# Loads, first projections, bias step and vector code of the attention phase rearranged in a two-layer gated transformer kernel

## What is computed

```
x = x + tanh(g_xattn[0]) * attention16(layernorm(x), ctx)      # 16 heads of 8
x = x + tanh(g_ffn[0])   * moe_silu(layernorm(x))              # 8 experts, top 2
x = x + tanh(g_xattn[1]) * bidaf(layernorm(x), ctx)            # trilinear attention
x = x + tanh(g_ffn[1])   * lora_moe_gelu(layernorm(x))         # 8 experts, top 2
```

## Time and profile before

| | us |
|---|---|
| median of 3 runs | 536.44 |
| lowest and highest run | 534.65, 537.83 |
| span of the profiled execution, first to last instruction | 534.4 |
| attention phase, from the start to the last `a_rec` | about 224 |

### The profile page before, as it was taken

The page is one execution under the profiler, slowest core; times in us unless marked ns, Lnnn a source line. Parts: engine busy times, 40 slices in busy tenths (PEclk is TensorE's granted clock), DMA queues, the critical chain, the costliest instruction groups (busy, mean ns, idle before and its releaser), DMA issues. The chain is left out here.

```text
span 534.4 us, 14733 instructions
## 1 busy us (share of the span) xinstructions
PE 487.3 (91%) x4456; PEld 394.8 (74%) x4456; DVE 420.5 (79%) x1690; ACT 316.8 (59%) x777; POOL 234.2 (44%) x328
## 2 busy tenths in 40 slices
PE   2688999998999989989999999998998999989997
PEld 1366777776767767777888888775887888779897
DVE  4788899999999969777766667685779995777973
ACT  1567877677776667545566665557553557454553
POOL 3322255545555465543330366541458864224420
PEclk9999999899999999999999999999999999999999
DMA  9603011000100121125675344331000112000011
GB/s 245 277 11 91 21 36 32 29 29 29 34 29 29 38 72 41 36 68 158 178 207 165 104 131 118 89 95 36 21 27 20 45 47 69 12 0 1 2 41 39
DMA packets 48129, 36.85 MB, mean 69 GB/s; under 512 B 6466, under 2 KB 43970, under 8 KB 47812
## 3 DMA queue, kind: packets, MB, share of 16 engines
q1 hardware_dynamic: 31332, 21.13, 13.3%
q0 software_dynamic: 4640, 9.45, 6.2%
q10 hardware_dynamic: 12096, 5.51, 3.7%
HBM read 22.44 MB, written 13.63 MB: 67 GB/s over the span
## 5 line engine op out<-in xcount | busy, mean ns | idle before, releaser
L474 POOL DMA_INDIRECT yg<-done,gidx x64 | 64.4, 1007 | 40.2 <-PE bank L1604 17.8
L1638 PE MATMUL bank<-QK 128*64 128x256 f32 x512 | 70.8, 399 | 11.1 <-DVE Pr L909 5.7
L458 POOL DMA_INDIRECT sent<-xr,rowu x60 | 58.9, 981 | 43.2 <-DVE rowu L1014 22.0
L440 POOL TENSOR_TENSOR ve<-mv,half 128x4 f32<-128x4 f32 (+1 forms) x40 | 8.9, 222 | 122.5 <-DVE mv L826 121.5
L1205 DVE TENSOR_TENSOR act<-sil,bank 128x256 f32<-128x256 f32 x80 | 33.6, 420 | 33.5 <-ACT sil L667 33.2
L617 ACT ACTIVATE PT<-bank 128x512 f32<-128x512 f32 x64 | 36.4, 602 | 35.7 <-PE bank L1604 34.9
L1638 PEld LDWEIGHTS bank<-QK 128*64 128x64 f32 x512 | 32.5, 139 | 29.8 <-DVE Pr L909 8.7
L667 ACT ACTIVATE sil<-bank 128x256 f32<-128x256 f32 x80 | 30.8, 384 | 39.4 <-PE bank L1794 39.4
L1810 PE MATMUL bank<-f0w_s,aT 128*128 x320 | 50.0, 279 | 0.7 <-DVE yb L1211 0.6
L905 DVE TENSOR_REDUCE mx<-bank 128x8 f32<-128x512 f32 x64 | 43.7, 682 | 4.2 <-PE bank L1638 4.0
L909 DVE TENSOR_TENSOR Pr<-bank,mx 128x512 f32<-128x512 f32 x64 | 43.7, 683 | 1.2
(11 more groups left out here) (237 smaller groups left out, 1323.0 us busy)
## 6 DMA issues: line engine op xcount, KB each, us to landing
xb<-sent SPq DMA_DIRECT2D x80, 64.0 KB
done<-yb ACTq DMA_DIRECT2D x80, 64.0 KB
cT<-ctx_t_dram SPq DMA_DIRECT2D x16, 128.0 KB, 2.1
f0w_s<-f_w_dram SPq DMA_DIRECT2D x1, 2048.0 KB, 11.1
Pr<-ctx_t_dram SPq DMA_DIRECT2D x8, 256.0 KB
QK<-ctx_tok_dram SPq DMA_DIRECT2D x8, 256.0 KB
out_dram<-xs SPq DMA_DIRECT2D x8, 256.0 KB, 2.3
xs<-x_dram SPq DMA_DIRECT2D x2, 512.0 KB, 5.7
```

Of the source, the lines that this page charges most:

```text
L458: nc.gpsimd.indirect_dma_start(sent, bass.IndirectOffsetOnAxis(ap=rowu[:, s, 2 * k + c:2 * k + c + 1], axis=0), rows[:, c, :], None).then_ ...
L474: nc.gpsimd.indirect_dma_start(yg[:, s, j, :], None, done[u // (U4 // HALVES)], bass.IndirectOffsetOnAxis(ap=gidx[:, s, j:j + 1], axis=0)) ...
L1638: last = mm(bank[g % 2][L * b:L * (b + 1), 256 * p:256 * (p + 1)], QT[:, s, g, t:t + L], Kb[:, s, :, t:t + L], start=True, stop=True)
```

## The change

1. **Loads.** SP loads two tiles of `x` first instead of four, then the constants, the context columns of unit 0, the next two tiles, the context columns of unit 1, the gates, eight tiles, and then the other small ones and the last twenty tiles. A new semaphore `ld_first` covers the constants, the bias columns and the weights of K and Q. ScalarE's queue loads the bias columns, then the weights of K, Q, V and O. The router's weights move from GpSimd's queue to SP's.
2. **Statistics** of the first four tiles are taken two by two, and GpSimd makes two small steps of them. `norm` of units 0 and 1 stands ahead of the preparations (`first_norm`).
3. **K of unit 0** is projected into bank 7 as soon as `ld_first` is there. ScalarE evicts K (`first_keys`), copies the transposed tiles, and evicts Q (`first_queries`), raising a semaphore for each of the four instructions; each group of scores of unit 0 waits for its own. The tanh of the gates follows behind them, and VectorE's preparations wait for it.
4. **Products that are never read** (`unread`, 128x512 in bfloat16, bank 6) are put on TensorE: eight at the start, then two, two and three between the first steps.
5. **The bias step.** The product of value bias and output weight goes from the very start to iteration -1, ahead of the fourth group of scores, and `split_biases` from iteration -3 to the end of iteration -1.
6. **VectorE's iterations** -3 to 15 are all straight code; its hardware loop is gone. The other engines keep theirs.

```diff
-X_FIRST = (0, 4, 12, 20, CH)
+X_FIRST = (0, 2, 4, 12, CH)
...
+            x_load(0)
+            sp.dma_start(cst[:], consts).then_inc(ld_first, 16)
+            first_columns(0)
+            x_load(1)
+            first_columns(1)
+            sp.dma_start(gate[:], gates.partition_broadcast(P)).then_inc(ld_small, 16)
+            x_load(2)
+            sp.dma_start(rowv[:], rows.partition_broadcast(P)).then_inc(ld_small, 16)
+            sp.dma_start(farf[:], far).then_inc(ld_small, 16)
+            sp.dma_start(f0g_s[:], f0_wg).then_inc(ld_small, 16)
+            x_load(3)
...
-            for w_s, w in ((wq_s, wq), (wk_s, wk), (wv_s, wv), (wo_s, wo)):
-                a.dma_start(w_s[:], w).then_inc(ld_attn, 16)
-            a.wait_ge(ld_small, 80)
-            nc.scalar.activation(tg[:], gate[:, 0:4], ACT.Tanh).then_inc(prep_act, 1)
+            a.dma_start(colv[:], cols).then_inc(ld_first, 16)
+            for w_s, w, signal in ((wk_s, wk, ld_first), (wq_s, wq, ld_first), (wv_s, wv, ld_attn), (wo_s, wo, ld_attn)):
+                a.dma_start(w_s[:], w).then_inc(signal, 16)
+            a.wait_ge(ld_first, 64)
...
+            def first_keys():
+
+                a.wait_ge(prep_pe, 1)
+                a.wait_ge(prep, 1)
+                a_ks(0, bank[7][:, 0:2 * P])
+
+            def first_queries():
+
+                a.wait_ge(S("a_qk"), 1)
+                a.wait_ge(fill, 11)
+                for g in range(NG):
+                    a_qs(0, g).then_inc(prep_act, 1)
...
-            a.wait_ge(prep, 3)
-            a.wait_ge(fill, 11)
+            first_keys()
+            a_xts(0)
+            first_queries()
+            a.wait_ge(ld_small, 64)
+            nc.scalar.activation(tg[:], gate[:, 0:4], ACT.Tanh).then_inc(prep_act, 1)
...
+            first_tiles(0)
+            v.wait_ge(ld_first, 64)
             nc.vector.tensor_scalar(bkm[:], cst[:, C_KM:C_KM + HG], colv[:, BK:BK + 1], None, ALU.mult).then_inc(prep, 1)
+            first_tiles(1)
+            first_norm(0)
+            first_norm(1)
+            v.wait_ge(ld_small, 64)
+            v.wait_ge(prep_act, NG + 2)
...
-                if isinstance(u, int) and u == -3:
-                    split_biases()
...
+                if isinstance(u, int) and u == -1:
+                    split_biases()
...
-            pipelined(v, it_a, -3, 3, UT, UA)
+            for u in range(-3, UA):
+                it_a(u, u % 2)
...
+            pe.wait_ge(fill, 8)
+            unread(6, 8)
+            pe.wait_ge(ld_first, 64)
+            pe.wait_ge(ld_cT[0], 16)
+            a_k(0, bank[7][:, 0:2 * P]).then_inc(prep_pe, 1)
+            unread(6, 2)
+            a_xt(0, 0)
+            unread(6, 2)
+            pe.wait_ge(S("a_xts"), 1)
+            a_q().then_inc(S("a_qk"), 1)
+            unread(6, 3)
...
+                if isinstance(u, int) and u == -1:
+                    output_bias()
```

More of the change, by code:

```diff
@@ L319, in has, with begun @@
             return not isinstance(u, int) or 0 <= u < units
+        def begun(u):
+            return isinstance(u, int) and u <= -2
         def pipelined(eng, it, first, loop, behind, end):
@@ L345, in _, with x_load, first_columns @@
         def _(sp):
[L346 to L354, removed]
+            def x_load(i):
                 some = slice(X_FIRST[i], X_FIRST[i + 1])
                 sp.dma_start(xs[:, some, :], x_v[:, some, :]).then_inc(ld_x[i], 16)
+            def first_columns(s):
+                sp.dma_start(cT[:, s, 0:2 * P], ctx_t[:, 2 * P * s:2 * P * (s + 1)]).then_inc(ld_cT[s], 16)
+            x_load(0)
[9 more added lines that the diff above has]
+            x_load(3)
             sp.dma_start(f0w12_s[:], f0_w12).then_inc(ld_f0, 16)
@@ L475, in fetch @@
                                                  bass.IndirectOffsetOnAxis(ap=gidx[:, s, j:j + 1], axis=0)).then_inc(back_s[s], 16)
-            with pool.Fori(0, U4) as u:
+            for i in range(2):
+                two = slice(2 * i, 2 * i + 2)
+                pool.wait_ge(S("mv0"), 1 + 2 * i + 2)
+                nc.gpsimd.tensor_tensor(ve[:, 0, two], mv[:, 0, two, 1], half[:, 0:1].to_broadcast([P, 2]), ALU.add).then_inc(S("ve0"), 1)
+                pool.wait_ge(S("ve0"), i + 1)
+                nc.gpsimd.tensor_tensor(ln[:, two, 1], ve[:, 0, two], half[:, 2:3].to_broadcast([P, 2]), ALU.pow).then_inc(S("ln0"), 1)
+            with pool.Fori(1, U4) as u:
                 rstd(0, u, 4)
@@ L597, in a_xts, with a_qs, a_ks @@
                 nc.scalar.activation(xT[:, 0, 0:2 * P], bank[4][:, 0:2 * P], ACT.Copy).then_inc(S("a_xts"), 1)
+            def a_qs(s, g):
+                rows_g = slice(32 * g, 32 * (g + 1))
+                return nc.scalar.activation(QT[rows_g, s, g, :], bank[4][rows_g, 0:2 * P], ACT.Identity, bias=bqs[rows_g], scale=float(DH) ** -0.5)
+            def a_ks(s, keys):
+                for j in range(HG):
+                    last = nc.scalar.activation(Kb[:, s, j, :], keys, ACT.Identity,
+                                                bias=bkm[:, j:j + 1], scale=cst[:, C_KM + j:C_KM + j + 1])
+                return last
             def a_qks(u, s):
@@ L637, in it_a @@
                     a_ats(u - 1)
-                if has(u + 2):
+                if has(u + 2) and not begun(u):
                     a_xts(u + 2)
@@ L1126, in it_a @@
                     r_keep(u - 3, 1 - s)
-                if has(u + 3):
+                if has(u + 3) and not begun(u):
                     wait(v, S("a_xt"), u + 2)
```

86 lines of the change are left out of this document (49 added, 37 removed).

## The result

The changed kernel takes **543.7 us** (median of 4 runs, 542.2 to 544.6) against 535.7 in the same session (4 runs, 534.65 to 537.83): ratio 1.0148, 95% interval 1.0123 to 1.0174. It is slower by 8 us, outside the range of the prediction. The profiled execution took 544.6, with a span of 542.8 us against 534.4 before.

What follows compares the result with a forecast made beforehand. VectorE was taken to set the pace in the attention loop, and its order to count at the start. Front +4.8 and loop -4.7 gave +0.1 us, so 536.5 us was forecast against a 536.4 median, range 532.5 to 540.6.

Steps and rivals of the forecast that it cites:

- the split: Bias split on VectorE, moved between unit 0's last subtraction and `norm` of unit 3: uncovered there, +2.9 us.
- The lower level behind the first gap: TensorE after idling before unit 0's third score group: slower third group, Q and K, +1.8 us.
- The bias product: TensorE makes it ahead of the fourth score group, for which VectorE already waited: +0.6 us.
- the earlier scores are worth nothing: Unit 0's scores start 7 us earlier, gaining nothing, since VectorE reads them only 7.03 us after starting statistics of tiles 4-7.
- the lower level behind the second gap: TensorE after idling 4 to 5 us before unit 1's third score group: priced 0, with 1.8 possible.
- The "unit" taken off for shared waits: Start of the attention phase, where TensorE and VectorE alternate: 0.7 us deducted from 5.5, giving +4.8.
- the front: Start of the attention phase: comes later by 4.8 us, bounds +2.7 and +8.2.
- TensorE starved at the front: Rival: TensorE at the lower level behind both gaps, between second and third score groups of units 0 and 1; 539.5, chance 0.17.
- the term of the loop: Attention loop: VectorE's straight code removes most of TensorE's 6.5 us of waiting, -4.7 us, bounds 2 and 6.5.
- The second weight: Small VectorE instruction in the loop: would mostly miss GpSimd's weight step and take 0.15 instead of 1.36 us.
- the wait for `att`: TensorE's short wait for VectorE in each loop iteration: about 0.22 us would remain, as in straight iterations.
- a shift of its end passes through: Behind the attention phase: nothing is changed there, so a shift of the phase's end reaches the kernel's end; no added cost.

Runs made afterwards that it cites:

- e2_straight_only: The kernel before the change with only VectorE's hardware loop written out as straight code; 533.98 us, ratio 0.9966.
- e1_loop_back: The changed kernel with VectorE's iterations 3 to 10 made a hardware loop again; 543.36 us, ratio 1.0152.

## Why the prediction was wrong

**What held.** The trace follows the steps for the first 32 us almost to the tenth. VectorE waits 3.46 until 12.07 for the tanh (forecast: 3 to 4, until about 12.4). The statistics of tiles 4 to 7 begin at 13.89 (14.1, in the bounds 13.7 to 14.6), the first maximum comes at 21.24 (near 21), and the split takes 29.53 to 32.46, 2.93 (2.9). TensorE idles 9.47 (more than 8) and its third group takes 1.98. `norm` of unit 3 stands at 32.46, where 32.4 was forecast. The lower level behind the first gap cost 2.0 by the run with that gap filled (1.8). The bias product took TensorE 0.59 (0.6), but with the gap filled it lengthened VectorE's wait for the fourth group only from 0.61 to 0.89; another 0.3, an idle stretch of VectorE among its statistics near 18.9 that the kernel before doesn't have, made up for it and was in no term. That the earlier scores are worth nothing in this order was right too, and so was that they aren't without value: the run with the scores first gets 5.7 us.

**The step that failed first: the lower level behind the second gap, taken as 0.** The prediction named the gap, of 4 to 5 us, and set its price to 0 with 1.8 as bound. It was 4.53 us long and cost 2.7. The nearest row was the gap of 3.94 in rows 8; I used it for the first gap and not for the second, which was longer than that row's. The row was weak evidence besides: Q took 1.22 ahead of it already, so in the kernel before TensorE had not yet been at its higher level and could lose nothing there. No row of before showed a gap of that size behind work at the higher level, and then both gaps should have carried the same price. Nor was the level seen only around gaps and at the start, as the prediction says: its own rows 2 have an iteration at 0.87. By the rule that I cited from the Trainium skill, page "TensorE: Matmul & The Clock Gate", section "Why this matters for your kernels", both gaps should pay, and both did: the measured 2.0 and 2.7 stand beside it. The "unit" taken off for shared waits, 0.7, was not found either: 5.6 had come by `norm`, the full sum. So the front cost 8.3 and not 4.8, just at the bound of 8.2 (whose terms, added up, give 8.0). That is the rival "TensorE starved at the front", to which I gave 0.17. Its 539.5 still set the full 4.7 of the loop against it. The range did nearly the same: its upper end joins the front's +8.2 with -4 from the loop, though the loop's own bound was -2. With that bound it would have reached 542.6. Part of the 8.3 may be luck of the pair: `e2_straight_only` has the code of before up to its first reciprocal, and from the statistics of tiles 4 to 7 to `norm` it takes 14.85 us where the kernel before took 13.01, since TensorE stayed longer at its lower level.

**The second step: the term of the loop, -4.7.** It measured -2.8 in its own iterations against `e1_loop_back`, and -1.8 in the medians of `e2_straight_only` with nothing else changed. The profiled execution shows -3.7, since in the kernel before one of these iterations also held a stretch at the lower level. Two assumptions failed. The second weight was to miss GpSimd's weight step "mostly"; it meets it in all eight iterations, at 1.69 to 1.96 us where 0.15 was forecast, and they take 12.4 to 12.7 and not 12.2. And the wait for `att` was to shrink to 0.22, the value of straight iterations; it is 0.43 in each. The sum's own lower bound, for a collision that goes on, was -2, and the sentence beside it on the Trainium skill's page "GPSIMD Engine Reference", section "1. Specifications", gave -2 to -3: near what was measured. L1029 has two inputs from SBUF, and its 1.69 beside GpSimd's 1.28 agrees with it.

**The third: "a shift of its end passes through".** With the front at +8.3 and the loop at -3.7 the kernel stood 4.6 late at the end of the loop, which is 541 and already just above the range. Another 1.7 comes from the lower level in a later iteration, and 2.1 behind the phase. The 2.1 look in the main like a spread between executions. From the last reciprocal to the end, where the kernels have the same code, the fourteen traces take 310.8 to 312.9 us; the kernel before has the lowest of them and the changed kernel the highest, and `e2_straight_only` takes 312.2 with the code of before. TensorE's waits for VectorE there are longer at three places, by 0.4, 0.4 and 0.7; the cause is open. Of the 1.7, the record shows only that a stretch at the lower level fell at 204.5 in the changed kernel. Those with the scores first, without the unread products and with the first gap filled have a long iteration there too, of 15.88, 15.88 and 15.75; the others take 14.2. Why it falls there stays open.

## What to carry to other kernels

Whether a producer's earlier result is worth anything is decided by the consumer's order: here 7 us of earlier scores brought nothing until the engine that reads them was made to read them first. A step moved off the start has to be priced twice, by its own time on the engine and by the gap that it opens on the engine that waits; a gap long enough to be followed by the lower level anywhere in the trace gets that price each time it occurs. Where such a gap can't be closed by order, products that nothing reads, placed in the gap and not ahead of it, are worth their place (4.7 us by the first reciprocal here), while such products ahead of it gave nothing that could be measured.

## What the runs showed of the hardware

- In the first 60 us of the fourteen traces, every idle gap of TensorE of 2.73 to 9.48 us behind its first products was followed by work at 1.2 GHz, and none of the gaps of 1.22 to 1.59 us was, where TensorE had been at 2.4 GHz. Behind gaps of 3.39, 4.08 and 4.47 us the next group still began at the higher level, and the level fell within it or behind it.
- The same gap doesn't always cost the same: 2.0 to 2.9 us for the first and 1.5 to 3.0 for the second, in traces with the same order around them.
- The lower level also comes where TensorE has only short waits: at 102.4 us in the kernel before, behind waits of 0.53 and 0.44, and at about 204.5 in the changed kernel, behind waits of 1.08 and 1.04. The kernel before has the last two as well, at 197.5 and 199.4, and its granted clock stays 1.00 there. Such a stretch in a costly place is worth 1.7 us, as much as a small edit.
- The granted clock in the windows reads 1.00 before the first change of level is recorded. Without the unread products the first scores took 1.97 where that column prints 1.00. At this kernel's start the durations tell the level, and that column doesn't.
- A 128x2 product on VectorE takes 0.15 us alone and 1.69 beside GpSimd's weight step, and ends with it; a 128x2 product with a column takes 0.22 alone and 1.97 there. With the register instructions gone, that meeting fell on the same instruction in all eight iterations.
